# Alternating GpSimd's gathers and putting additions between its indirect DMAs

## The reference

```
x = x + attn(layernorm(x))      # linear attention, 8 heads, plus a 5-tap convolution of v, times a gate
x = x + ffn(layernorm(x))       # mixture of experts, 8 experts, top 2
# ffn: probs = softmax(x @ gate_w.T); the two largest; out = sum over both of
#      prob * (silu(x @ w1[e] + b1[e]) @ w2[e] + b2[e])
```

## Time and profile before

| | us |
|---|---|
| median of three timed runs | 554.52 |
| lowest and highest | 551.62 and 557.63 |
| span of the profiled execution, first to last instruction | 604.2 |
| busy: TensorE, VectorE, GpSimd, ScalarE | 513.4, 441.4, 361.1, 302.2 |

### The profile page before, as it was taken

The page is one execution under the profiler, slowest core; times in us unless marked ns, Lnnn a source line. Parts: engine busy times, 40 slices in busy tenths (PEclk is TensorE's granted clock), DMA queues, the critical chain, the costliest instruction groups (busy, mean ns, idle before and its releaser), DMA issues. The chain is left out here.

```text
span 604.2 us, 10225 instructions
## 1 busy us (share of the span) xinstructions
PE 513.4 (85%) x2821; PEld 408.8 (68%) x2821; DVE 441.4 (73%) x1396; ACT 302.2 (50%) x671; POOL 361.1 (60%) x322
## 2 busy tenths in 40 slices
PE   2999899999999999967794699889999988992982
PEld 2778777777777778756673478767777866871761
DVE  6788888878888886764773488668788876881774
ACT  2445333333333333234882577567667755761752
POOL 3332467777777776876017102888788788855361
PEclk9999899999999997967898799999999998996896
DMA  8627968858888511164266487879889988993653
GB/s 281 198 71 232 356 242 295 292 179 293 293 292 299 211 39 33 39 237 145 88 232 239 158 292 248 253 241 277 256 268 298 301 265 250 308 319 94 224 165 119
DMA packets 65609, 134.77 MB, mean 223 GB/s; under 512 B 8208, under 2 KB 24976, under 8 KB 60560
## 3 DMA queue, kind: packets, MB, share of 16 engines
q1 hardware_dynamic: 51984, 116.79, 54.6%
q0 software_dynamic: 13568, 17.32, 12.4%
HBM read 29.83 MB, written 63.09 MB: 154 GB/s over the span
## 5 line engine op out<-in xcount | busy, mean ns | idle before, releaser
L894 POOL DMA_INDIRECT rows_in<-yrow,slots x128 | 125.4, 980 | 63.3 <-issue 34.8
L1444 DVE TENSOR_TENSOR hl<-hf,hh 128x512 fp32r<-128x512 f32 x156 | 108.6, 697 | 18.9 <-ACT hh L857 13.9
L1442 DVE CAST hh<-hf 128x512 fp32r<-128x512 f32 x144 | 64.0, 445 | 52.9 <-ACT hf L853 41.9
L853 ACT ACTIVATE hf<-qp,wst 128x512 f32<-128x512 f32 x104 | 72.4, 696 | 54.5 <-PE qp L495 29.8
L952 POOL DMA_INDIRECT xres<-rows_out,slots x48 | 78.3, 1632 | 14.6 <-issue 14.6
L943 POOL DMA_INDIRECT yrow<-rows_out,slots x40 | 40.5, 1013 | 55.9 <-DMA rows_out<-yo 38.9
L753 ACT ACTIVATE yrow<-xres,nb,rs 128x128 f32<-128x128 f32 x64 | 26.3, 482 | 63.6 <-DVE nb L1123 63.6
L853 ACT ACTIVATE hf<-kvp,wst 128x512 f32<-128x512 f32 x52 | 36.1, 695 | 41.1 <-PE kvp L495 18.2
L493 PE MATMUL qp<-xT_h,wst 128*128 128x512 f32 x104 | 46.2, 445 | 2.4 <-DVE xT_l L1402 1.8
L488 PE MATMUL gate_wo<-first_sb,yTs 128*128 128x128 f32 x156 | 25.7, 291 | 26.1 <-ACT yTs L865 24.3
L902 POOL TENSOR_TENSOR rs<-ve,half 128x8 f32<-128x8 f32 x20 | 33.8, 1690 | 23.4 <-DVE ve L1006 22.6
(11 more groups left out here) (224 smaller groups left out, 1440.6 us busy)
## 6 DMA issues: line engine op xcount, KB each, us to landing
wst<-wres SPq DMA_DIRECT2D x39, 1030.5 KB
rows_out<-tail SPq DMA_DIRECT2D x28, 1280.0 KB
xg<-rows_in SPq DMA_DIRECT2D x39, 272.0 KB
rows_out<-yo SPq DMA_DIRECT2D x39, 256.0 KB
wraw<-in_w_experts SPq DMA_DIRECT2D x8, 512.0 KB, 4.3
out_x<-xres SPq DMA_DIRECT2D x16, 256.0 KB
rows_in<-tail SPq DMA_DIRECT2D x11, 272.0 KB, 4.0
rows_in<-yrow,slots POOLq DMA_INDIRECT x128
```

What stands on the lines that cost most here:

```text
L853: nc.scalar.activation(hf[n % N_H][:], hbank(t, c), ACT.Silu, bias=b_part(wst[t % NBUF], c, 1)).then_inc(s["h_silu"], 1)
L894: nc.gpsimd.indirect_dma_start(rows_in, bass.IndirectOffsetOnAxis(ap=slots[:, f, k, j:j + 1], axis=0), rows_of(f)[:, j, :], None).then_inc ...
L1442: nc.vector.tensor_copy(hh[n % N_H][:], hf[n % N_H][:]).then_inc(s["h_high"], 1)
L1444: nc.vector.tensor_tensor(hl[n % N_H][:], hf[n % N_H][:], hh[n % N_H][:].bitcast(F32), ALU.subtract).then_inc(s["h_low"], 1)
```

## The change

A tile `spacer` of 128 x 384 floats is set to zero at the start. A helper `space` waits for the last operation on it and adds it to itself on GpSimd. Blocks 13 to 15 are scattered in pairs of DMAs with one `space` behind each pair, four a block. In `gather` the two loops become one: the gather of the second choice and that of the first alternate, for all blocks; in the last four blocks one `space` follows each such pair, four a block.

```diff
+        spacer = sb("spacer", [P, 3 * P])
...
             pool.wait_ge(s["ones_set"], 1)
+            nc.gpsimd.memset(spacer[:], 0.0).then_inc(s["spaced"], 1)
             nc.gpsimd.memset(tail[:], 0.0).then_inc(s["tail_set"], 1)
...
             spreads(NB + 1, (NB + 1) % 2)
+            spaces = [1]
+
+            def space():
+
+                pool.wait_ge(s["spaced"], spaces[0])
+                nc.gpsimd.tensor_tensor(spacer[:], spacer[:], spacer[:], ALU.add).then_inc(s["spaced"], 1)
+                spaces[0] += 1
+
             for f in range(NB - 3, NB):
-                to_experts(f, 0)
-                to_experts(f, 1)
+                for k in range(TOP_K):
+                    to_experts(f, k, range(SUB // 2))
+                    space()
+                    to_experts(f, k, range(SUB // 2, SUB))
+                    space()
...
                         bass.IndirectOffsetOnAxis(ap=slots[:, b, 1, j:j + 1], axis=0)).then_inc(s[f"got1_{b % N_GOT}"], 16)
-                for j in range(SUB):
                     if plain(b):
                         nc.gpsimd.indirect_dma_start(
                             first_got[b - NB + LAST_PLAIN][:, j, :], None, rows_out,
                             bass.IndirectOffsetOnAxis(ap=slots[:, b, 0, j:j + 1], axis=0)).then_inc(s[f"got0_{b % N_GOT}"], 16)
+                        space()
                         continue
```

More of the change, by code:

```diff
@@ L277, in build @@
             clear_in got0_0 got0_1 got0_2 got0_3 got0_4 got0_5 got0_6 got0_7 got0_8
-            got1_0 got1_1 got1_2 got1_3 got1_4 got1_5 got1_6 got1_7 got1_8 first_added combined out_in""".split()
+            got1_0 got1_1 got1_2 got1_3 got1_4 got1_5 got1_6 got1_7 got1_8 first_added combined out_in spaced""".split()
         s = {n: sem(n) for n in names}
```

## The result

| | before | after |
|---|---|---|
| median of the timed runs shown together, us | 553.07 (551.3 to 557.63) | 568.5 (565.34 to 569.18) |
| ratio | | 1.0251, interval 1.0211 to 1.0291 |
| span of the profiled execution, us | 604.2; a second one of the same kernel 552.1 | 566.3 |

The changed kernel is 15 us slower by the medians and 13.9 (11.7 to 16.1) by the ratio, as forecast. That the forecast time is the measured one to the tenth is luck: the way to it was not right in all steps, and two misses nearly cancelled.

The account below looks back on a forecast made before the run. The prediction took GpSimd's line to end the timed run, with TensorE's 4 us apart and the profile's stalls mostly absent. 554.5 + 5 (late scatters) + 9 (last blocks) = 568.5 us, range 546 to 580.

Parts of the forecast that it names:

- The late scatters: Blocks 14 and 15: 7 additions delay the last scatter 6.2 us, SyncE waits at tile step 8; 5 us taken.
- stall 1: Expert stage, first profile, between 322 and 336 us: 12.9 us lost, ScalarE late, inside the run of 16 scatters.
- The last blocks: Blocks 12 to 15: 15 additions ahead of the last gather, 13.2 us in full; 9 taken because the lines are close.
- The rebuilt lines: Timed run rebuilt from the first profile without stalls: span 560.9 by GpSimd's line, 556.5 by TensorE's, 4 us apart.
- undisturbed pace: GpSimd's gathers before the last four blocks: 12.3 us a block, 148 us for 12 blocks, against 157.6 in the profile.
- I take the coincidence as cause: Expert stage: the longest runs of cheap indirect DMAs on GpSimd hold ScalarE up during profiling, 25.4 us together.
- Mostly a trait of the profiled execution: Expert stage: the ScalarE stalls, 25.4 us, cannot stand in full in the timed runs, given the 49.7 us.
- rival A: Expert stage: the stalls are in the timed runs too and the change removes 13 us, giving 541; chance 0.2.
- The span may well fall while the time rises: Whole kernel: profiled span about 582 if the additions break up the runs and both stalls vanish, timed median 568.5.
- B: Last blocks and late scatters: GpSimd has room, so the additions cost 0 to 4 us, time 556; chance 0.17.
- C: Expert stage: additions and VectorE's `hl` subtractions collide, 22 additions cost 0.35 us more each, time 576; chance 0.08.
- Alternating at nothing: Gathers of 12 blocks: changing kinds costs under 3 us of GpSimd's line, covered by the spread of the lines.

Follow-up runs that it names:

- before_again: The kernel before, unchanged, profiled a second time: 553.93 us, span 552.1.
- alt_only: The kernel before with only the two kinds of gather alternating, no additions: 553.5 us, ratio 0.9976.
- memset_all: The changed kernel with a memset of the same length in place of each addition: 565.9 us, ratio 1.02 to the kernel before.
- plain7: The kernel before with seven blocks gathered plainly at the end instead of four: 547.11 us, ratio 0.9871.
- gath_double: The changed kernel without additions among the scatters, and two additions instead of one behind each pair of late gathers: 586.17 us, ratio 1.0593 to the kernel before.
- gath_two_tiles: gath_double with every second addition on another tile, so none waits for the one just ahead: 577.8 us, ratio 1.0449 to the kernel before.
- scat_behind: The kernel before with eight additions behind the last late scatter and none ahead of it: 556.26 us, ratio 1.0053.

## Why the prediction was right, and where it was wrong

**The direction and the mechanism were right.** GpSimd is the later line, and additions in it are paid at the end. The last gathers stand without a wait of 10 us, and VectorE's last two additions wait for gathers:

```profile
559.31 1.03 DVE L1434 TENSOR_TENSOR xres<-xres,more_got 128x512 f32<-128x512 f32 x1 [10.89 <-DMA more_got<-rows_out,slots]
560.55 0.69 DVE L1438 TENSOR_TENSOR xres<-xres,first_got 128x512 f32<-128x512 f32 x1 [0.21 <-DMA first_got<-rows_out,slots]
```

Each addition costs 0.72 us where 0.88 was taken; the instruction itself is 0.84, below the 0.9 to 1.1 named as a sign.

**The late scatters: 5 us taken, 3.6 measured.** 5 lies at the upper end of what was measured (2.2 to 5.0). The scatters take 28.6 instead of 21.9 us from the first to the last, 6.7 more, near the 6.2 of the prediction and for two reasons: 7 x 0.72 = 5.0, and the 16 scatters themselves take 17.8 us instead of 16.1, which the prediction put at nothing. "Almost no cover is left" was right, though worked out from a SyncE at 351.66 less stall 1: in the second profile SyncE stands waiting for the last scatter before the change already. What the step didn't have is that the last scatter, issued later, lands sooner behind its issue (1.35 us instead of 3.8; why stays open), so that SyncE is only 3.8 us later, and VectorE's hold-up, a second price beside the first.

**The last blocks: 9 us taken, 11.2 measured.** "Below the full price because the lines are close" is the failed step here. 13.2 was the full price by 0.88; the true full price is 10.8, and all of it is paid, since the lines are not close. The rebuilt lines put the last gather's end (561.3 less stall 1, 548.4) at 1.1 us behind TensorE's last group (595.02 less 34.8 and stall 1, 547.3); in the second profile it is 13.4 us behind that group, and making GpSimd's line 7.2 us cheaper gained 7.2. The term that was mis-sized is GpSimd's "undisturbed pace": 12 blocks at 12.3 us, 148 us, in place of the 157.6 that the first profile had. Without any stall they take 157.9 in the second profile and 156.8 in the changed kernel: 12.3 was worked out from the shortest gathers, 0.94 and 1.54 us, and not from their means, 1.03 and 1.65 in the second profile. TensorE's pace was right: 29 tiles were put at 186.5 us and took 185.7. Both rebuilt lines began some 15 us too late, since the first profile had lost that much before its late scatters. Too high a price and too small a share of it nearly cancelled, and so did the misses in the two stretches: 5 + 9 = 14 forecast, 3.6 + 11.2 = 14.8 measured.

**"I take the coincidence as cause" was wrong.** The stalls of the earlier trace rows lay in the two longest runs of cheap indirect DMAs, and I let these runs make them. `before_again` and `alt_only` have runs as long, and neither has such stalls. "Mostly a trait of the profiled execution" was right, and it carried the forecast: had the stalls been in the timed runs, rival A's 541 would have been due. The Trainium skill's rule on the block that collects trace records, "NOTIFIC — the notification-queue block", section "7.1 Overflow: three behaviours, one of which stalls the engine", stays untested: the second profile took as many records of the same kernel without losing time.

**"The span may well fall while the time rises"** came true (604.2 to 566.3) for another reason than the one given: the next execution had no such stalls, with the additions or without. It fell below the 582 named.

**The rivals.** A falls with `before_again`. B falls: GpSimd doesn't idle before blocks 13 to 15. C was right that additions and VectorE collide, and its sign, a longer `hl`, came: in the changed kernel GpSimd's additions stay at 0.83 to 0.85 us, and `hl` grows from 0.69 to as much as 1.89. Its price, 7.7 us, did not. How much of the hold-up is on the path in the last blocks was not measured by itself; the memsets of `memset_all` say that it is little in all, and behind the scatters it was worth 0.5%. The rule that the prediction cited for C is on the Trainium skill's page "SBUF — State Buffer", section "Who interferes with whom", and the traces agree with it: `hl` beside an addition takes up to 1.95 us, beside a memset 0.69.

**Alternating at nothing** was right (0.9976).

## What to carry to other kernels

When a profile's span is far off the timed median, take a second profile before reading its waits: here it was the distance of 49.7 us, and no row of the stalls themselves, that spoke against stalls in the timed runs. Work filled in on an engine is free only until its line is the last one; whether it is shows best by making the line cheaper, as `plain7` did, since that gains just what it saves, up to where the next line ends the run. In `gath_double` an instruction that waited for its own predecessor also held back the small register work behind it, which otherwise ran ahead unseen.

A line that is rebuilt from the shortest times of its instructions comes out too short: here by 10 us, which hid the lead of GpSimd's line.

## What the runs showed of the hardware that was not expected

A GpSimd addition of 128 x 384 floats, 0.84 us, held up the VectorE instruction beside it by as much as 1.2 us (`hl`, 1.89 instead of 0.69, in the changed kernel). Two additions that follow each other without a wait held up one VectorE instruction through both. In `gath_two_tiles`, beside additions from 514.18 to 515.79, an addition that takes 0.69 us elsewhere:

```profile
513.86 2.50 DVE L1449 TENSOR_TENSOR xres<-xres,yrow 128x512 f32<-128x512 f32 x1
```

Casts with one input from SBUF are held up as well: `hh`, 0.43 us, takes 1.05 beside the additions of `scat_behind`, and 1.23 beside a memset in `memset_all`. Memsets of the same length leave `hl` at 0.69.

GpSimd's register loads of a block's numbers take 0.3 to 0.6 us each, and with the work around them 2.6 us for block 13 in `gath_double`. In `gath_two_tiles` they ran ahead, beside the gathers of the block before; in `gath_double`, where an addition in front of them stood waiting, they didn't. Taking that wait out made the difference between 1.0593 and 1.0449.
